# Attention scores and maxima in two float32r parts with two heads in the row halves of the array, in place of three bfloat16 parts with one head at a time

## The reference

```
x  = x + softmax((x Wq + bq)(c Wk + bk)^T / 4) (c Wv + bv)          # 77 context tokens c
x  = x + (softmax(q k^T / 4) v) Wo + b,   q, k, v from LN1(x)       # self-attention, 1024 keys
x  = x + (softmax(q k^T / 4) v) Wo + b,   q from LN2(x), k, v from c
x  = x + gelu(LN3(x) W1 + b1) W2 + b2                               # 256 -> 1024 -> 256
```

## Time and profile before

| | us |
|---|---|
| three runs | 842.11, 835.05, 838.48 |
| median | 838.48 |
| profiled execution, first to last instruction (the page has no other time of it) | 836.5 |
| TensorE matmuls busy | 749.0 |
| VectorE busy | 530.3 |
| ScalarE busy | 452.1 |
| GpSimd busy | 164.8 |

### The profile page before, as it was taken

How to read it: one execution, slowest core, us unless ns; L and a number is a source line. 1 busy time by engine, 2 the same in 40 slices (tenths; PEclk the granted TensorE clock), 3 DMA queues, 4 the chain that set the end, 5 groups by cost and what they waited for, 6 DMA issues and landing times.

```text
span 836.5 us, 11551 instructions
## 1 busy us (share of the span) xinstructions
PE 749.0 (90%) x4182; PEld 338.4 (40%) x4224; DVE 530.3 (63%) x836; ACT 452.1 (54%) x826; POOL 164.8 (20%) x355
## 2 busy tenths in 40 slices
PE   6677896589999999999999999997989897999998
PEld 3333444235222222222333333332444453556767
DVE  3445978475888888888878878874457767140001
ACT  4355553245776777777666666666644645422120
POOL 7312362364000000000000101223123214030000
PEclk9779899698999999999999999999999999999999
DMA  8967515992014060511406001004261730000001
GB/s 268 187 176 130 124 41 147 120 163 74 2 23 56 1 77 2 64 15 24 54 1 77 2 2 23 20 21 90 48 155 48 143 45 2 1 1 25 26 13 38
DMA packets 43769, 52.82 MB, mean 63 GB/s; under 512 B 9344, under 2 KB 29760, under 8 KB 43712
## 3 DMA queue, kind: packets, MB, share of 16 engines
q1 hardware_dynamic: 43424, 51.99, 32.7%
q10 hardware_dynamic: 288, 0.08, 0.1%
HBM read 36.31 MB, written 15.15 MB: 62 GB/s over the span
## 4 chain that ended last, share of the span: by engine, by line
PE 72%; DMA 11%; DVE 7%; ACT 4%; issue 3%; SPq 2%; POOL 1%; another core or an unknown queue 0%; ACTq 0%; DVEq 0%; POOLq 0%
PE PV L742 18%; PE ST L728 15%; PE SM L675 12%; PE ST L641 5%; PE ST L637 5%; DMA stacks<-mrow 3%; DMA stacks<-q_parts 3%; DVE nm L949 3%; PE SM L628 3%; PE SM L618 2%; DMA q_parts<-split 2%; PE SM L622 2%; PE PV L641 2%; PE PV L637 2%; PE SM L680 2%
## 5 line engine op out<-in xcount | busy, mean ns | idle before, releaser
L843 ACT ACTIVATE prob<-ST 128x512 f32<-128x512 f32 (+1 forms) x640 | 346.2, 598 | 180.9 <-PE ST L728 152.0
L949 DVE TENSOR_REDUCE nm<-SM 128x1 f32<-128x1024 f32 x256 | 303.0, 1220 | 65.4 <-PE SM L675 64.2
L728 PE MATMUL ST<-stacks 128*128 128x512 bf16 (+1 forms) x598 | 204.7, 391 | 20.7 <-DMA stacks<-mrow 13.9
L742 PE MATMUL PV<-prob,Vst 128*32 128x512 f32 x1280 | 174.8, 619 | 3.1 <-ACT prob L843 2.8
L675 PE MATMUL SM<-stacks 96*128 96x512 bf16 x512 | 153.2, 383 | 23.0 <-DMA stacks<-q_parts 14.3
L728 PEld LDWEIGHTS ST<-stacks 128*128 128x128 bf16 (+1 forms) x640 | 57.1, 101 | 206.6 <-ACT prob L843 141.7
L952 DVE TENSOR_REDUCE nm<-SM 128x4 f32<-128x308 f32 x128 | 58.3, 473 | 47.9 <-PE SM L680 47.2
L675 PEld LDWEIGHTS SM<-stacks 96*128 96x128 bf16 x512 | 47.9, 98 | 80.6 <-DVE nm L949 20.1
L1116 POOL CAST mp<-nm 128x16 bf16<-128x16 f32 x48 | 9.6, 199 | 356.3 <-DVE nm L949 249.2
L905 DVE TENSOR_TENSOR X<-ST,X 128x256 f32<-128x256 f32 x18 | 7.5, 423 | 90.5 <-PE ST L641 73.7
L742 PEld LDWEIGHTS PV<-prob,Vst 128*32 128x32 f32 x1280 | 25.5, 109 | 62.8 <-ACT prob L843 34.7
(11 more groups left out here) (102 smaller groups left out, 674.3 us busy)
## 6 DMA issues: line engine op xcount, KB each, us to landing
stacks<-q_parts SPq DMA_DIRECT2D x144, 128.0 KB, 5.7
q_parts<-split SPq DMA_DIRECT2D x24, 384.0 KB, 4.3
stacks<-k_parts SPq DMA_DIRECT2D x48, 128.0 KB, 7.5
k_parts<-split SPq DMA_DIRECT2D x8, 384.0 KB, 3.8
fm<-in_xT SPq DMA_DIRECT2D x4, 512.0 KB, 7.9
X<-in_x SPq DMA_DIRECT2D x4, 512.0 KB, 5.2
V<-in_w SPq DMA_DIRECT2D x2, 1024.0 KB, 9.0
out<-X SPq DMA_DIRECT2D x16, 128.0 KB, 1.7
```

The lines of the kernel that those rows point to most:

```text
L728: mm(ST[0:att.keys, n % 3, :], keys_of(att, g, h, kt), QST[att.name][g % att.buffers][:, h, j * BLK:(j + 1) * BLK], start=True, stop=True) \
L742: last = mm(PV[h * 32:(h + 1) * 32, :], Vst[:, g % 2, kt, h, :], prob[:, t % 2, h, :], start=(kt == 0), stop=(kt == att.kt - 1))
L843: act_fn(prob[0:att.keys, t % 2, h, :], ST[0:att.keys, n % 3, :], ACT.Exp) \
L949: ins = vec.tensor_reduce(nm[:, q % 2, v // QUAD, v % QUAD:v % QUAD + 1], ps, AX.X, ALU.max, negate=True)
```

## The change

Queries and keys are split into two float32r parts (a 4-byte type of fewer mantissa bits that TensorE takes in one instruction) instead of three bfloat16 parts, and three products of parts are kept. Three bands of 16 rows and two rows for the maxima make 50 rows, so a head fits in half of the array's rows: even heads sit in partitions 0 to 63, odd heads in 64 to 127, and scores and maxima of two heads are issued as pairs into different banks. The diff, cut to what is spoken of:

```diff
-PARTS = 3
+PARTS = 2
-BANDS = [(0, 0), (0, 1), (0, 2), (1, 0), (1, 1), (2, 0)]
+BANDS = [(0, 0), (0, 1), (1, 0)]
+SIDES = 2                       # side buffers of two banks each, in all three attentions
+CTXP = CTX + 1                  # 78: an even number of keys, the last one twice
-    q_parts = nc.dram_tensor("q_parts", [3, PARTS, BATCH * DIM, SEQ], BF16).ap()
+    q_parts = nc.dram_tensor("q_parts", [3, PARTS, BATCH * DIM, SEQ], FP32).ap()
-        stacks = sb("stacks", [P, A1.buffers, 2, QUAD, SEQ], BF16)
+        stacks = sb("stacks", [P, A1.buffers, 2, PAIR, SEQ], F32R)
...
                 for band, (kpart, qpart) in enumerate(BANDS):
-                    rows = slice(band * HD, (band + 1) * HD)
...
+                    for side in range(2):
+                        rows = slice(side * HALF + band * HD, side * HALF + (band + 1) * HD)
...
                     sp.wait_ge(*READ[w])
-                    sp.dma_start(QST[att.name][g % att.buffers][SROWS:MROWS, :, j * BLK:(j + 1) * BLK],
-                                 mrow[:, q % 2, :]).then_inc(rows_in[q % 2], 16)
+                    for c in range(QUAD):
+                        side, n = divmod(c, PAIR)
+                        rows = slice(side * HALF + SROWS, side * HALF + MROWS)
+                        sp.dma_start(QST[att.name][g % att.buffers][rows, n, j * BLK:(j + 1) * BLK].bitcast(FP32),
+                                     mrow[c * PARTS * TPB:(c + 1) * PARTS * TPB, q % 2, :].bitcast(FP32)) \
+                          .then_inc(rows_in[q % 2], 16)
...
                     if att.whole:
-                        h = v % QUAD
-                        for c in range(SEQ // BLK):
-                            last = mm(ps[:, c * BLK:(c + 1) * BLK], Q[0:SROWS, h, c0:c0 + P], ...)
+                        tile, n, c = v // 4, v // 2 % 2, v % 2
+                        for s in range(2):
+                            rows = slice(s * HALF, s * HALF + SROWS)
+                            last = mm(ps[:, s * BLK:(s + 1) * BLK], Q[rows, n, c0:c0 + P],
+                                      Kst[g % att.buffers][rows, n, c * BLK:(c + 1) * BLK], start=True, stop=True)
...
-                    for n in range(TPB):
-                        last = nc.tensor.transpose(ps.bitcast(BF16)[0:PARTS * QUAD, n * P:(n + 1) * P], ...)
+                    last = nc.tensor.transpose(ps[:, 0:P], mp[:, which % 2, :].bitcast(FP32), ident[:, :])
...
+                    rows = slice(h % 2 * HALF, h % 2 * HALF + MROWS)
                     mm(ST[0:att.keys, n % 3, :], keys_of(att, g, h, kt),
-                       QST[att.name][g % att.buffers][:, h, j * BLK:(j + 1) * BLK], start=True, stop=True) \
+                       QST[att.name][g % att.buffers][rows, h // 2, j * BLK:(j + 1) * BLK], start=True, stop=True) \
...
-                    for h in range(QUAD):
-                        if t < att.steps:
+                    for n in range(PAIR):
+                        for h in range(2 * n, 2 * n + 2) if t < att.steps else []:
                             scores(t, h)
+                        if n == 1 and 1 <= t <= att.steps:
+                            values(t - 1)
                         for slot, w in work:
-                            if slot == h:
+                            if slot // 2 == n:
                                 side(att, w)
-                        if h == 1 and 1 <= t <= att.steps:
-                            values(t - 1)
...
-            def first_part(w): ...      # ScalarE: first part
-            def second_part(w): ...     # ScalarE: second part
+            def high(w, ps):            # ScalarE, from PSUM, in the step of the product
+                if n >= SB:
+                    act.wait_ge(parts_stored[n % SB], 16 * (n // SB))
+                act_fn(split[:, n % SB, 0, 0:width], ps[:, 0:width], ACT.Identity, bias=cols[:, c:c + 1])
...
-                            act_fn(prob[...], ST[0:att.keys, n % 3, :], ACT.Exp)
+                            act_fn(prob[...], ST[0:att.keys, n % 3, :], ACT.Exp, scale=SCALE)
...
-                    return vec.tensor_scalar(q32[:, n % SB, 0:width], ps[:, 0:width], ...)
+                    dve.wait_ge(high_ready, n + 1)          # VectorE: second part, from PSUM
+                    return vec.scalar_tensor_tensor(split[:, n % SB, 1, 0:width], ps[:, 0:width], cols[:, c:c + 1],
+                                                    split[:, n % SB, 0, 0:width].bitcast(FP32), ALU.add, ALU.subtract)
-            def rest(w): ...            # VectorE and GpSimd: subtract the first part
-            def third_part(w): ...      # VectorE and GpSimd: subtract the second part
```

More of the change, by code:

```diff
@@ L13 @@
-import numpy as np
+import itertools
 import concourse.bass as bass
@@ L18 @@
 FP32 = mybir.dt.float32
-BF16 = mybir.dt.bfloat16
+F32R = mybir.dt.float32r
 ALU = mybir.AluOpType
@@ L471, in load @@
                 sp.dma_start(tile, src.rearrange("(k p) n -> p k n", p=P)).then_inc(done, 16)
-            load(ctxT[:, :, :], cT_d, in_k0)
+            for b in range(BATCH):
+                load(ctxT[:, :, b, 0:CTX], cT_d[:, b * CTX:(b + 1) * CTX], in_k0)
             load(w_k0[:, :, :], wk0, in_k0)
@@ L574, in attention @@
                         side(w)
-                    for w in att.products(t - att.lag[1]):
+                    for w in att.products(t):
                         if w[0] in SPLITS:
@@ new lines, in side @@
+                        c0 = j * BLK + tile * P
+                        for s in range(2):
+                            rows = slice(s * HALF, s * HALF + SROWS)
+                            last = mm(ps[:, s * BLK:(s + 1) * BLK], Q[rows, n, c0:c0 + P],
+                                      Kst[g % att.buffers][rows, n, c * BLK:(c + 1) * BLK], start=True, stop=True)
+                    else:
+                        b, n0 = g // QUAD, (g % QUAD) * PAIR
+                        for tile, n, s in itertools.product(range(2), range(PAIR), range(2)):
+                            c0 = j * BLK + (2 * v + tile) * P
+                            at = s * BLK + (tile * PAIR + n) * CTXP
+                            rows = slice(s * HALF, s * HALF + SROWS)
+                            last = mm(ps[:, at:at + CTXP], Q[rows, n, c0:c0 + P],
+                                      Kc[rows, n0 + n, b * CTXP:(b + 1) * CTXP], start=True, stop=True)
@@ L998, in between @@
                         chore((stage, tb, *more))
-                    elif stage in SPLITS:
-                        if ring_split_by(stage, tb) == BOTH_DVE:
-                            for w in block_of(stage, tb, *more):
-                                rest(w)
-                            for w in block_of(stage, tb, *more):
-                                third_part(w)
-                    elif stage in READER and stage != "up":
+                    elif stage in SPLITS or stage in READER and stage != "up":
                         for w in block_of(stage, tb, *more):
@@ L1170, in between @@
                         rsqrt(int(stage[-1]), tb)
-                    elif stage in SPLITS and ring_split_by(stage, tb) == BOTH_POOL:
-                        for w in block_of(stage, tb, *more):
-                            rest(w)
-                        for w in block_of(stage, tb, *more):
-                            third_part(w)
             def attention(att):
```

353 lines of the change are left out of this document (138 added, 215 removed).

## The result

The changed kernel takes 953.69 us (median of 4 runs, 948.97 to 975.09) against 838.88 for the kernel before on the same chip: a ratio of 1.137, 95% interval 1.131 to 1.142. The prediction said 815, in 765 to 868: wrong in sign. The profiled execution after spans 947.2 us, 110.7 more than before.

The account below looks back on a forecast made before the run. The prediction took a1 to be bound by TensorE, with VectorE close behind. Opening -2, splits -9, a1 -10 and -12, a0 and a2 +10 sum to -23, so 838.5 becomes 815 us, in a range of 765 to 868.

Parts of the forecast that it names:

- float32r at 0.22, a pair at the price of one: Scores and maxima: a 512-column float32r matmul takes 0.22 us, as in bfloat16, and two heads side by side also take 0.22.
- Rivals 2 and 3: Scores and maxima: float32r streams at 0.43, some 880 us (chance 0.11); row halves run one after the other, 857 (0.13).
- The rows' transfers: a1, each block's first score: four issues of 0.43 to 0.72 us, leaving a wait of 1.2 to 2.5 a block.
- Rival 1: SyncE's queue and each block's first score: the rows' transfers become the bound, 860 us; chance 0.14.
- A step of 2.6: a1: VectorE bounds a step at 2.5 us, 2.6 with slack, before the wait for rows makes it 2.88.
- a1 itself: a1, taken as 200.9 to 588 us: -10 in the first 198.8 us and -12 in the other 188.3.
- Splits, -9: Between the last product before a1 and a1's stack: shorter splits let the stack issue near 134 instead of 141, -9 us.
- a0 and a2, +10: a0 and a2: weight loads +5, paired scores -5, queued rows' transfers +10; together +10 us, between -10 and +38.
- The weight load: a0 and a2, 16 maximum matmuls a step: 0.11 us each, +0.2 a step, +5 us over 32 steps.
- Opening, -2: Before a0, full of loads with DMA at 0.98: -2 us, between 0 and -8.
- Feed-forward, 0: From 712.5 us to the end, TensorE alone: the change leaves it as it is, 0 us.
- A switch of tiling: a0 and a2: by the skill's drain rule, two more switches in each of 32 steps add up to 13 us, giving 828.

## Why the prediction was wrong

- **The step that failed** is one it never worked out: every duration was taken at the clock of the earlier trace rows, as if TensorE's share could fall from 2.9 to 2.0 a step at no price. It treated the idle time that the change makes as harmless. The runs put 43 us of a1 (52 less the waits' 8.7) on the clock. In a0 and a2 the price is an estimate: by the mean clocks a0 spent 79 us at half clock and a2 40, before 16 and 7; a step of 6.41 for 3.98 loses 0.38 of its time there, so the added 96 us of half clock, all priced like that, cost some 36 of the 47. The Trainium skill, TensorE: Matmul & The Clock Gate, section The HAM clock gate, says that the gate follows how busy TensorE has been; the prediction didn't weigh it. By the waits the trace agrees; by the busy column it doesn't: 65.67 of 66.00 at 0.50 in a0.
- **float32r at 0.22, a pair at the price of one**: right in row halves, 0.23. Rivals 2 and 3 are out. Over the whole array a float32r matmul of 512 columns takes 0.33 in these runs (two in 0.66).
- **The rows' transfers**: right in place, a little high: 0.65 an issue for 0.43 to 0.72, some 0.9 a block waited for 1.2 to 2.5. Rival 1 had the loss on this step, but by the transfers' own time.
- **A step of 2.6**: reached (2.66) only with the maxima moved; as written it is 2.90. I carried over the slack of the step before and didn't follow the new order from the first exponential back to itself. With the rows earlier a1 is still 8.5 us longer than before; with the maxima moved too it is 25 shorter.
- **a1 itself** was cut too short: around 588 a2's maxima begin (585.2). a1's scores run on to 613, and a2's first score starts at 618.31, so the forecast was made for 387 of some 417 us.
- **Splits, -9**: from the last product's end to a1's first maximum TensorE takes 18.3 us (160.0 to 178.3) instead of 28.3, so the term was right. The stage as a whole is only 4 shorter (68.7 for 72.4): from that maximum to the first exponential it takes 51.1 for 45.7, and why, no run separates.
- **a0 and a2, +10** in -10 to +38: +47. The weight load was not the cause (eight maxima in 0.64 at full clock, as two bfloat16 groups of four in 0.31 each). Nor were the waits for rows, which carried the +10: inside a0 there are none, inside a2 2.3 us, before 4.7 and 3.2. (The 4.07 and 6.55 of the earlier trace rows are links of the chain of waits; TensorE itself stood for 3.0 at the longest.) Half clock has some 36 by the estimate above; the rest fits the longer step at full clock, 3.98 for 3.47, but isn't shown to be that.
- **Opening, -2**: +5.6; TensorE waits 10.1 us for the rows of a0's first block, 6.0 before. **Feed-forward, 0**: +1.
- **A switch of tiling**: the prediction priced two more switches in each of 32 steps at up to 13 us. With the maxima first the next pair starts at 376.58, 0.99 after the values that began at 375.59, and the values take 1.06 as in the earlier trace rows; that pair takes 0.34 to the next where later ones take 0.23, so a switch costs 0.11 at most here. The Trainium skill, TensorEngine Tiling (Array Packing), section Key Properties, says that changing the tiling mode drains TensorE; no run here shows a drain longer than that.

## What to carry to other kernels

Where a change lightens TensorE, ask what its clock will do: look for the longest wait left in a step's circle, and for a stage whose matmuls all run in part of the array, and price the stage at half clock as a rival. Follow the circle of one step by hand, from the first consumer back to itself, before dividing busy times. And take a change apart by stage: a1's part, with its order mended, was worth 28 us; with a0 and a2 changed as well the kernel takes 55 us more (865.68 for 810.28).

## What was not expected of the hardware

- Waits of about 1 to 2.4 us cost the kernel before, whose scores are whole-array bfloat16, nothing or some 3 us of half clock each; shorter ones of 0.8 to 1.0 cost the changed kernel, with float32r pairs in row halves, 3 to 41 us each.
- Two float32r matmuls a step over 128 rows held 1.00 through ten waits of a1; over 48 rows, same count, columns and busy share, the clock fell behind six of ten.
- Half clock at a busy share near 1.00 can last most of a stage (a0: 65.67 of 66.00 us, 54 to 120).
